# Attention and residual kernel on one core: how the inverse softmax sums reach the layout of the values product

## The chip, the cores and the metric

The kernel runs on one core of one Trainium2 chip. The metric is the device time of one execution in microseconds (us); lower is better. The engines are named as in the profile: PE (TensorE, with PEld for its weight loads), DVE (VectorE), ACT (ScalarE), POOL (GpSimd) and SP (SyncE, which issues the DMAs).

## The reference

The input x has 4 batches of 1024 rows of 1024. Rows are normalised (RMS), scaled and shifted from a condition, multiplied by `W_qkv`, and split into 16 heads of 64. What matters here is the attention of a head:

```python
q = _rms_norm(q, g_q)
k = _rms_norm(k, g_k)
logits = jnp.einsum('bhqd,bhkd->bhqk', q, k) * d ** (-0.5)
attn = jax.nn.softmax(logits, axis=-1)
o = jnp.einsum('bhqk,bhkd->bhqd', attn, v)
o = jnp.swapaxes(o, 1, 2).reshape(b, n, dim)
return o + o @ W_out
```

The result is added to x, a causal convolution of 4 taps over the rows follows with its own residual, and that is the output. The kernel applies the division of the softmax after the product with v: each row q of a head is multiplied by the inverse of its sum of exponentials. The change concerns only the path of these inverses.

## The kernel before, in words

After a short preparation (weights scaled and split into two fp16 halves) the work runs in U = 32 **units**, one for each batch and pair of heads, numbered u = 0 to 31. Every large product is made of three fp16 products, of high and low halves. A unit has 8 **steps** p; step p treats 128 query rows of both heads. In a step:

- PE makes the scores of the two heads (`score`, L958), 128 x 1024 each, into two halves of the PSUM tile `scores`. It waits there until ACT has read the scores of the step before (`exp_done`).
- DVE takes the row maxima (`maximum`, L1558) and from them the bias (L1561), for one head after the other.
- ACT takes the exponentials with their row sums in `total` (`exponent`, L1201), both heads, and then the high halves (`high`, L1209), both heads.
- DVE makes the low halves (`low`, L1567), both heads, and SP transposes the pair by DMA into `pT` (L762).

Two steps form a **group** g = 0 to 3 (256 rows of two heads, four columns of sums: two blocks of rows `a` times two heads `h`). When a group's probabilities are transposed, PE multiplies them with v (`attend`, L977, in two parts of 24 matmuls each). Its output is `values[:, 0:256]` in PSUM: the 64 columns of a head lie on 64 partitions, the 256 query rows along the free dimension. So the inverses, which DVE has with the query rows on partitions (`inv`, 128 x 4), have to be turned and repeated over the 64 partitions of each head. Before the change this goes as follows, for each of the 128 groups:

1. `invert` on DVE, at steps p = 2, 4 and 6 (and p = 0 of the next unit): reciprocal (L1668), scaled high half in fp16 (L1671), low half (L1673), in `inv_pair`.
2. `inverses` on PE, at the next odd step: two fp16 transposes (L992) into 4 partitions of `values`, seen as fp16.
3. `inverse_rows` on ACT, at the start of the same odd step: copy of 4 x 256 to `inv_row` (L1269). The first part of `attend` on PE waits for it (`inv_ev`).
4. The second part of `attend`, one step later, ends with one matmul more (L984): the 0/1 matrix `sel` (4 x 128) times `inv_row` adds the halves and repeats each head's row over its 64 partitions, in `values[:, 256:512]`.
5. `read_inverses` on ACT, at even steps between the exponentials and the high halves: 128 x 256 to `inv_all` (L1275).
6. `scale_values` on DVE, just before `low`: `oT = values * inv_all` (L1682). ACT and POOL split `oT` into halves (L1285, L1503), and SP stores them.

What else a unit carries is placed by the same hand-written order on each engine. PE makes the q, k and v products of unit u + 1 in pieces (`project`, L1016, four or five steps of a unit) with transposes of the halves of q and k (`stacks`, L1028), and from unit 8 on the products with `W_out` of unit u - 8 (`out_product`, L1050, with L1056 adding x) and float32 transposes of the result (`out_transposes`, L1068, four at a time). DVE normalises q and k (L1589, L1593), and from unit 8 on does the convolution (L1707, L1710, L1714). POOL does powers (L1474) and low halves (L1479, L1488, L1503). In units 1 to 7 PE has little beside the attention in steps 5 to 7; from unit 8 on it has a `W_out` product there. Each engine runs its own instructions in the written order, and waits in it hold everything behind them.

The functions that the diff touches follow.

## Time and profile before

| what | value |
|---|---|
| median of 3 runs (each: 2477.67, 2477.79, 2483.67) | 2477.79 us |
| span of the profiled execution, first to last instruction | 2476.2 us |
| PE busy | 2362.7 us (95%), 20794 matmuls |
| DVE busy | 2089.6 us (84%) |
| ACT busy | 1825.8 us (74%) |
| POOL busy | 641.1 us (26%) |
| PE on the chain that ended last | 64% |
| DVE on that chain | 20% |

The profiled execution's time as a run is not listed apart; its span is 1.5 to 1.6 us below the two runs that agree, which is what lies around the span. Busy times are sums over all stages. The page adds for each engine where in the span it is busy, the chain of work that ended last, and the groups of instructions with their mean durations. Matmuls overlap their successors, so the duration of one (0.2 to 0.4 us) is longer than the step from one to the next; the steps are read from the chain and the timeline.

### The profile page before, as it was taken

The page shows a single profiled execution, that of the slowest core. Times are in us where ns is not written, and L with a number is a line of the kernel's source. Part 1 is how long each engine was busy: PE and PEld are TensorE (multiplying, and loading weights), DVE is VectorE, ACT ScalarE, POOL GpSimd, SP SyncE. Part 2 cuts the span into 40 slices and gives each one's busy share as a digit, 9 for nine tenths or more (in the row PEclk, how much of TensorE's full clock was granted, in tenths as well). Part 3 has the DMA queues.
Part 4 walks back from the last instruction along what each step waited for, and adds up shares of the span by engine and source line. Part 5 has one row for each costly group of instructions (what it writes and reads, how often), then busy time and mean ns, then how long its engine had stood idle before and what let it go on. Part 6 is the DMA issues. An engine that isn't in the chain of part 4 may idle for free.

```text
span 2476.2 us, 54245 instructions
## 1 busy us (share of the span) xinstructions
PE 2362.7 (95%) x20794; PEld 1524.8 (62%) x20794; DVE 2089.6 (84%) x3368; ACT 1825.8 (74%) x2834; POOL 641.1 (26%) x451
## 2 busy tenths in 40 slices
PE   4799998999899999999999999999999999999899
PEld 0455555555466666666666666666666666666688
DVE  7769888888778888888888888888888888888876
ACT  5477778888777777877777787777777777777732
POOL 1132232332233222333332223233212222221100
PEclk9899999999999999999999999999999999999999
DMA  9999999999998989999999999999988888889971
GB/s 360 311 217 223 192 183 194 180 193 224 201 196 181 197 182 213 181 199 223 201 213 182 210 186 196 184 191 228 202 174 170 180 172 163 171 166 173 182 188 52
DMA packets 1234737, 484.99 MB, mean 196 GB/s; under 512 B 1139632, under 2 KB 1197872, under 8 KB 1232048
## 3 DMA queue, kind: packets, MB, share of 16 engines
q1 hardware_dynamic: 1234480, 481.53, 92.4%
q8 instruction: 166, 2.72, 0.5%
q14 instruction: 91, 0.75, 0.1%
HBM read 137.20 MB, written 56.66 MB: 78 GB/s over the span
## 4 chain that ended last, share of the span: by engine, by line
PE 64%; DVE 20%; issue 5%; ACT 4%; SPq 2%; DMA 1%; POOL 0%; ACTq 0%; POOLq 0%
PE proj L1016 33%; PE scores L958 10%; DVE neg L1558 9%; PE values L977 9%; PE proj L1050 8%; DVE p_pair L1567 7%; ACT p_pair L1209 3%; DVE bias L1561 2%; PE proj L1056 1%; PE misc L1068 1%; SPq L762 1%; ACT late L1201 1%; DMA w_sb<-w_dram 1%; PE values L992 1%; PE values L984 1%
## 5 line engine op out<-in xcount | busy, mean ns | idle before, releaser
L1016 PE MATMUL proj<-w_sb,xn_sb 128*128 128x384 f16 x6144 | 1035.2, 327 | 20.8 <-DMA w_sb<-w_dram 13.2
L1201 ACT ACTIVATE late<-scores,bias,l_scale 128x1024 f32<-128x1024 f32 x512 | 615.6, 1203 | 344.9 <-DVE bias L1561 325.8
L1016 PEld LDWEIGHTS proj<-w_sb,xn_sb 128*128 128x128 f16 x6144 | 587.2, 98 | 425.4 <-issue 25.9
L1567 DVE TENSOR_TENSOR p_pair<-late,p_pair 128x1024 f16<-128x1024 f32 x512 | 616.2, 1245 | 124.9 <-ACT p_pair L1209 124.8
L1558 DVE TENSOR_REDUCE neg<-scores 128x1 f32<-128x1024 f32 x512 | 623.0, 1217 | 107.0 <-PE scores L958 103.6
L1209 ACT ACTIVATE p_pair<-late 128x1024 f16<-128x1024 f32 x512 | 510.9, 1050 | 0.0
L977 PE MATMUL values<-pT,v_pair 128*64 128x256 f16 x6144 | 389.7, 277 | 14.6 <-ACT inv_row L1269 14.6
L958 PE MATMUL scores<-late 64*128 64x512 f16 x3072 | 376.1, 378 | 15.0 <-ACT late L1201 12.9
L977 PEld LDWEIGHTS values<-pT,v_pair 128*64 128x64 f16 x6144 | 319.0, 111 | 94.1 <-issue 70.3
L1474 POOL TENSOR_TENSOR rs<-ms,power 128x16 f32<-128x16 f32 x63 | 183.1, 2906 | 404.1 <-DVE ms L1581 403.7
L1050 PE MATMUL proj<-late,wo 128*128 128x256 f16 x2304 | 267.7, 273 | 1.3 <-issue 1.3
L1503 POOL TENSOR_TENSOR oT_pair<-oT,oT_pair 128x256 f16<-128x256 f32 x124 | 144.4, 1164 | 461.0 <-ACT oT_pair L1285 461.0
L958 PEld LDWEIGHTS scores<-late 64*128 64x128 f16 x3072 | 128.9, 94 | 195.7 <-issue 45.6
L1050 PEld LDWEIGHTS proj<-late,wo 128*128 128x128 f16 x2304 | 220.5, 98 | 31.5 <-issue 1.6
L1479 POOL TENSOR_TENSOR qk_pair<-stage,qk_pair 128x512 f16<-128x512 f32 x126 | 145.4, 1174 | 330.4 <-ACT qk_pair L1232 330.4
L1714 DVE SCALAR_TENSOR_TENSOR late<-late,taps 128x256 f32<-128x256 f32 x324 | 157.1, 485 | 11.6
L1217 ACT ACTIVATE stage<-proj 128x384 f32<-128x384 f32 x256 | 122.2, 477 | 29.8 <-PE proj L1016 29.8
L1269 ACT ACTIVATE inv_row<-values 4x256 f16<-4x256 f16 x128 | 46.9, 366 | 119.2 <-PE values L992 119.2
L1561 DVE TENSOR_SCALAR bias<-neg,l_scale 128x1 f32<-128x1 f32 x512 | 109.7, 214 | 18.1
L1499 POOL TENSOR_TENSOR pair<-x_in,pair 128x1024 f16<-128x1024 f32 x24 | 66.2, 2757 | 206.5 <-ACT pair L1263 199.5
L1201 ACT ACTIVATION_READ_ACCUMULATOR late<-scores,bias,l_scale 128x1 f32 x512 | 98.5, 192 | 0.0
L1050 PE MATMUL proj<-xn_sb,wo 128*128 128x256 f16 x744 | 86.5, 273 | 1.2 <-ACT late L1307 1.2
(183 smaller groups left out, 2023.6 us busy)
## 6 DMA issues: line engine op xcount, KB each, us to landing
w_sb<-w_dram SPq DMA_DIRECT2D x121, 384.0 KB, 4.1
o_dram<-oT_pair SPq DMA_DIRECT2D x124, 128.0 KB, 2.4
out<-late SPq DMA_DIRECT2D x54, 256.0 KB, 2.9
x_in<-in_x SPq DMA_DIRECT2D x25, 512.0 KB, 4.6
late<-in_x SPq DMA_DIRECT2D x25, 512.0 KB, 4.1
wq_raw<-in_L_cond_W_qkv SPq DMA_DIRECT2D x8, 1536.0 KB, 11.2
late<-o_dram SPq DMA_DIRECT2D x12, 1024.0 KB, 6.1
xn_dram<-late SPq DMA_DIRECT2D x21, 512.0 KB, 3.6
```

Of the source, the lines that this page charges most:

```text
L958: last = nc.tensor.matmul(scores[:, h, n * HN:(n + 1) * HN], stack[rows_, par, i, p * P:(p + 1) * P], stack[rows_, par, j, n * HN:(n + 1) ...
L977: last = nc.tensor.matmul(values[DH * h:DH * h + DH, 0:QG].rearrange("p (a n) -> p a n", a=2), v_pair[:, par, 2 * c + h, DH * i:DH * i + D ...
L1016: last = nc.tensor.matmul(proj[:, t % 2, 0:6 * DH], xn_sb[:, t, i * K + c, :], w_sb[:, c, j, :], start=(c == 0 and i == j == 0), stop=(c = ...
L1050: last = nc.tensor.matmul(dst, const["wo"][:, c, b, m * P:(m + 1) * P], oT_[:, c, a, :], start=(c == 0 and a == b == 0 and c1 == K), stop= ...
L1201: nc.scalar.activation(prob[:, h, :], scores[:, h, :], ACT.Exp, bias=bias[:, s:s + 1], scale=const["l_scale"][:, 0:1], accum_out=total[:, ...
L1209: nc.scalar.activation(p_pair[:, s % 4, 0, :], prob[:, h, :], ACT.Copy).then_inc(hi_done, 1)
L1474: nc.gpsimd.tensor_tensor(rs[:], ms[:], const["power"][:, 0:4 * KH], ALU.pow).then_inc(h_pw, 1)
L1479: last = nc.gpsimd.tensor_tensor(qk_pair[:, j, 1].rearrange("p t (h d) -> p (t h) d", d=DH), stage[:, hf, :, j * DH:(j + 1) * DH], qk_pair ...
L1558: nc.vector.tensor_reduce(neg[:, s:s + 1], scores[:, h, :], axis=AX.X, op=ALU.max, negate=True).then_inc(max_done, 1)
L1561: nc.vector.tensor_scalar(bias[:, s:s + 1], neg[:, s:s + 1], const["l_scale"][:, 0:1], P_SHIFT, ALU.mult, ALU.add).then_inc(bias_done, 1)
L1567: nc.vector.tensor_tensor(p_pair[:, s % 4, 1, :], prob[:, h, :], p_pair[:, s % 4, 0, :], ALU.subtract).then_inc(lo_done, 1)
L1714: nc.vector.scalar_tensor_tensor(out=acc_[:, m, :], in0=y_[:, m, k:k + QG], scalar=const["taps"][:, k, c:c + 1], in1=acc_[:, m, :], op0=AL ...
```

## The change

DVE copies the four float32 inverses of a group into `inv_wide`, each repeated over 64 columns (128 x 256, one instruction with a broadcast source). PE turns this with two float32 transposes of 128 x 128 straight into `values[:, 256:512]`, where each head's 64 partitions now hold its row. ACT reads that to `inv_all` where it read the 4 x 256 before, and `attend` waits for this read. The halves (L1671, L1673), the copy of the rows (L1269) and the product with `sel` (L984), and the `sel` matrix itself, are gone, and `inv_all` no longer has a read of its own between exponentials and high halves.

```diff
--- before.py
+++ after.py
@@ -72,7 +72,6 @@
             wo=sb("wo", [P, K, 2, D], F16),
             eps_u=sb("eps_u", [P, U], F32),
             back=sb("back", [P, U], F32),
-            sel=sb("sel", [4, 2 * DH], F16),
             y_scale=sb("y_scale", [P, U], F32),
             carry=sb("carry", [P, U], F32),
             g_qk=sb("g_qk", [P, DH], F32),
@@ -399,10 +398,6 @@
             nc.vector.tensor_copy(smallT[:], ps_mod[:, 0:rows]).then_inc(small_c, 1)
             v.wait_ge(small_c, 1)
             v.wait_ge(eyed, 1)
-            step(nc.vector.tensor_tensor(
-                const["sel"][:].rearrange("p (h d) -> p h d", d=DH),
-                const["eye32"][0:4, 0:2].rearrange("p (h a) -> p h a", a=1).to_broadcast([4, 2, DH]),
-                const["eye32"][0:4, 2:4].rearrange("p (h a) -> p h a", a=1).to_broadcast([4, 2, DH]), ALU.add))
             step(nc.vector.tensor_copy(const["taps"][:], smallT[:, 0:B * K].rearrange("p (b c) -> p b c", c=K)))
             step(nc.vector.tensor_scalar(const["taps"][:, B - 1, :], const["taps"][:, B - 1, :], 1.0, None, ALU.add))
             step(nc.vector.tensor_copy(const["conv_b"][:], smallT[:, row_cb:rows]))
@@ -474,7 +469,6 @@
     QG = 2 * P
     TAPS = B
     H = TAPS - 1
-    INV_UP = 2.0 ** 22
     x_t = x.rearrange("b n d -> (b n) d")
     out_t = out.rearrange("b n d -> (b n) d")
     wo_v = W_out.rearrange("(c p) n -> c p n", p=P)
@@ -497,8 +491,7 @@
         v_pair = sb("v_pair", [P, 2, 2 * K, 2 * DH], F16)
         p_pair = sb("p_pair", [P, 4, 2, N], F16)
         inv = sb("inv", [P, 2, 4], F32)
-        inv_pair = sb("inv_pair", [P, 2, 2, 4], F16)
-        inv_row = sb("inv_row", [4, QG], F16)
+        inv_wide = sb("inv_wide", [P, 2, 2, P], F32)
         inv_all = sb("inv_all", [P, QG], F32)
         oT = sb("oT", [P, QG], F32)
         oT_pair = sb("oT_pair", [P, 2, QG], F16)
@@ -586,11 +579,8 @@
         pT_in = [sem(f"pT_in{i}") for i in range(8)]
         pv_done = sem("pv_done")
         inv_rc = sem("inv_rc")
-        inv_hi = sem("inv_hi")
         inv_done = sem("inv_done")
         inv_tr = sem("inv_tr")
-        inv_ev = sem("inv_ev")
-        all_mm = sem("all_mm")
         all_ev = sem("all_ev")
         o_done = sem("o_done")
         o_hi = sem("o_hi")
@@ -662,8 +652,6 @@
         first_pair = [p_pair[:, i] for i in range(4)]
         square = x_in
         last_y = scores[:, 0, 0:QG]
-
-        inv_bank = values[0:4, QG:QG + P].bitcast(F16)
 
         def odd_tail(T):
             return static(T) and T >= U - K - 1 and T % 2 == 1
@@ -965,7 +953,7 @@
             def attend(u, g, par, part):
                 n = NG * u + g
                 if part == 0:
-                    pe.wait_ge(inv_ev, n + 1)
+                    pe.wait_ge(all_ev, n + 1)
                     if g == 0:
                         pe.wait_ge(v_lo, 2 * u + 2)
                     for i in range(4):
@@ -981,16 +969,14 @@
                                 start=(c == 0 and i == j == 0), stop=(c == K - 1 and j == 1))
                 if part == 1:
                     last.then_inc(pv_done, 1)
-                    nc.tensor.matmul(values[:, QG:2 * QG], const["sel"][:], inv_row[:],
-                                     start=True, stop=True).then_inc(all_mm, 1)
 
             def inverses(u, g):
                 n = NG * u + g
                 pe.wait_ge(inv_done, n + 1)
                 need(pe, o_done, n)
                 for a in range(2):
-                    last = nc.tensor.transpose(inv_bank[:, a * P:(a + 1) * P], inv_pair[:, g % 2, a, :],
-                                               const["eye16"][:])
+                    last = nc.tensor.transpose(values[:, QG + a * P:QG + (a + 1) * P], inv_wide[:, g % 2, a, :],
+                                               const["eye32"][:])
                 last.then_inc(inv_tr, 1)
 
             def project(w, t, q0, q1, fins=None):
@@ -1262,18 +1248,11 @@
                 else:
                     nc.scalar.activation(pair_[:, 0], buffer, ACT.Copy).then_inc(x_hi, 1)
 
-            def inverse_rows(u, g):
+            def read_inverses(u, g):
                 n = NG * u + g
                 act.wait_ge(inv_tr, n + 1)
-                need(act, all_mm, n)
-                nc.scalar.activation(inv_row[:], inv_bank, ACT.Copy).then_inc(inv_ev, 1)
-
-            def read_inverses(u, g):
-                n = NG * u + g
-                act.wait_ge(all_mm, n + 1)
                 need(act, o_done, n)
-                nc.scalar.activation(inv_all[:], values[:, QG:2 * QG], ACT.Copy,
-                                     scale=1.0 / INV_UP).then_inc(all_ev, 1)
+                nc.scalar.activation(inv_all[:], values[:, QG:2 * QG], ACT.Copy).then_inc(all_ev, 1)
 
             def o_high(u, g):
                 n = NG * u + g
@@ -1329,9 +1308,9 @@
                     if last and p == 4:
                         read_y(T, T - par + 2, 1)
                     if p % 2 == 1 and p >= 3:
-                        inverse_rows(u, (p - 3) // 2)
+                        read_inverses(u, (p - 3) // 2)
                     elif p == 1 and begun:
-                        inverse_rows(u - 1, 3)
+                        read_inverses(u - 1, 3)
                     if p == 0:
                         if has_early(u):
                             read_projection(w, 1)
@@ -1361,10 +1340,6 @@
                         read_projection(w + 1, 0)
                     exponent(u, p, 0, par)
                     exponent(u, p, 1, par)
-                    if p % 2 == 0 and p >= 4:
-                        read_inverses(u, (p - 4) // 2)
-                    elif p % 2 == 0 and begun:
-                        read_inverses(u - 1, 2 + p // 2)
                     high(u, p, 0)
                     high(u, p, 1)
                     if 4 <= u < K and p in (1, 3):
@@ -1441,17 +1416,15 @@
             high_values(0, 0, 1)
             in_units(unit, act)
             scales = U - K + 2
-            read_inverses(U - 1, 2)
             read_y(U - K, scales, 0)
             read_y(U - K, scales, 1)
             o_high(U - 1, 2)
             read_y(U - K + 1, scales, 0)
-            inverse_rows(U - 1, 3)
+            read_inverses(U - 1, 3)
             read_out(U - K - 1, 0)
             read_y(U - K + 1, scales, 1)
             read_out(U - K - 1, 1)
             read_out(U - K, 0)
-            read_inverses(U - 1, 3)
             o_high(U - 1, 3)
             for T in range(U - K + 2, U):
                 read_y(T, scales, 0)
@@ -1667,12 +1640,9 @@
                 col = par * NS + 4 * g
                 nc.vector.reciprocal(inv[:, g % 2, :], total[:, col:col + 4]).then_inc(inv_rc, 1)
                 dve.wait_ge(inv_rc, n + 1)
-                one_ = inv[:, g % 2, :].rearrange("p (a h) -> p a h", a=2)
-                nc.vector.tensor_scalar(inv_pair[:, g % 2, :, 0:2], one_, INV_UP, None, ALU.mult).then_inc(inv_hi, 1)
-                dve.wait_ge(inv_hi, n + 1)
-                nc.vector.scalar_tensor_tensor(out=inv_pair[:, g % 2, :, 2:4], in0=one_, scalar=INV_UP,
-                                               in1=inv_pair[:, g % 2, :, 0:2], op0=ALU.mult,
-                                               op1=ALU.subtract).then_inc(inv_done, 1)
+                by_row = inv[:, g % 2, :].rearrange("p (a b) -> p a b", b=1).to_broadcast([P, 4, DH])
+                nc.vector.tensor_copy(inv_wide[:, g % 2].rearrange("p a (h d) -> p (a h) d", d=DH),
+                                      by_row).then_inc(inv_done, 1)
 
             def scale_values(u, g):
                 n = NG * u + g
```

In the order of PE's instructions, in a unit of the second half of the program: L977 and L965 are the values product of before and now, L958 and L946 the scores, L1016 and L1002 the q, k, v product, L1068 and L1054 the float32 transposes of the result, L992 and L978 the transposes of the inverses. Before:

```order
L958 MATMUL scores<-late 128x512 x12
L977 MATMUL values<-pT,v_pair 64x256 x24
L984 MATMUL values<-inv_row,sel 128x256
L1016 MATMUL proj<-w_sb,xn_sb 128x384 x36
L1068 MATMUL misc<-eye,late 128x128 x4
L958 MATMUL scores<-late 128x512 x12
L992 MATMUL values<-eye,inv_pair 4x128 x2
L1050 MATMUL proj<-late,wo 128x256 x24
```

Now:

```order
L946 MATMUL scores<-late 128x512 x12
L965 MATMUL values<-pT,v_pair 64x256 x24
L1002 MATMUL proj<-w_sb,xn_sb 128x384 x36
L1054 MATMUL misc<-eye,late 128x128 x4
L946 MATMUL scores<-late 128x512 x12
L978 MATMUL values<-eye,inv_wide 128x128 x2
L1036 MATMUL proj<-late,wo 128x256 x24
```

The `sel` product between the values product and the projection is gone, and the two transposes of the inverses give 128 partitions in place of 4; nothing else moved.

In the order of ACT's instructions, steps 0 and 1 of a unit (L1201 and L1187 are the exponentials, L1209 and L1195 the high halves, L1285 and L1264 the high half of `oT`). Before:

```order
L1201 ACTIVATE late,total<-scores,bias,l_scale 128x1024 x2
L1275 ACTIVATE inv_all<-values 128x256
L1209 ACTIVATE p_pair<-late 128x1024 x2
L1285 ACTIVATE oT_pair<-oT 128x256
L1217 ACTIVATE stage<-proj 128x384
L1269 ACTIVATE inv_row<-values 4x256
L1217 ACTIVATE stage<-proj 128x384
L1201 ACTIVATE late,total<-scores,bias,l_scale 128x1024 x2
L1209 ACTIVATE p_pair<-late 128x1024 x2
L1263 ACTIVATE pair<-x_in 128x1024
```

Now:

```order
L1187 ACTIVATE late,total<-scores,bias,l_scale 128x1024 x2
L1195 ACTIVATE p_pair<-late 128x1024 x2
L1264 ACTIVATE oT_pair<-oT 128x256
L1203 ACTIVATE stage<-proj 128x384
L1255 ACTIVATE inv_all<-values 128x256
L1203 ACTIVATE stage<-proj 128x384
L1187 ACTIVATE late,total<-scores,bias,l_scale 128x1024 x2
L1195 ACTIVATE p_pair<-late 128x1024 x2
L1249 ACTIVATE pair<-x_in 128x1024
```

The read of `inv_all` stands where the copy to `inv_row` stood, and nothing stands between the exponentials and the high halves.

## Rows read from the trace of the kernel before

**Rows 1.** Busy us in units 9 to 30 by engine (PE, PEld, DVE, ACT, POOL), clock, DMA.
```profile
738.30:2311.40 1573.10, 1571.68 (x14168) 1031.12 (x14166) 1360.55 (x2180) 1214.01 (x1905) 433.96 (x294) 1.00 0.94 189
```

**Rows 2.** The chain, units 15 and 16: start us, length us, what.
```profile
1205.86 0.21 PE values L984
...
1212.02 0.44 PE misc L1068 x4
...
1213.86 0.20 PE values L992 x2
...
1217.24 2.62 PE proj L1050 x24
...
1220.31 0.45 PE misc L1028 x8
...
1236.01 1.47 PE scores L958 x12
...
1307.55 1.47 PE scores L958 x12
```

**Rows 3.** Timeline, TensorE near the end: start us, us, instruction, idle before.
```profile
2387.38 0.66 PE L1068 MATMUL misc<-eye,late 128*128 128x128 f32 x4
2387.97 1.50 PE L977 MATMUL values<-pT,v_pair 128*64 128x256 f16 x24
```

**Rows 4.** Groups by line: shapes, count, busy us, mean ns, idle before and releaser.
```profile
L1275 ACT ACTIVATE inv_all<-values 128x256 f32<-128x256 f32 x128 | 47.6, 372 | 1.0 <-PE values L984 1.0
L1269 ACT ACTIVATE inv_row<-values 4x256 f16<-4x256 f16 x128 | 46.9, 366 | 119.2 <-PE values L992 119.2
...
L1707 DVE TENSOR_SCALAR late<-late,taps,conv_b 128x256 f32<-128x256 f32 x108 | 43.9, 407 | 0.0
```

**Rows 5.** The tile inv_pair: durations in ns, least, median, most.
```profile
L1671 DVE TENSOR_SCALAR inv_pair<-inv x128: 169/169/1143, 156.6 to 2372.9; 128x4 f16<-128x4 f32 x128
L1673 DVE SCALAR_TENSOR_TENSOR inv_pair<-inv,inv_pair x128: 161/163/1076, 156.8 to 2373.1; 128x4 f16<-128x4 f32 x128
```

**Rows 6.** Timeline of unit 15 from step 6 on, to the first scores of the next.
```profile
1222.56 0.98 PEld L958 LDWEIGHTS scores<-late 64*128 64x128 f16 x12 [0.20 <-issue]
...
1225.25 2.27 POOL L1479 TENSOR_TENSOR qk_pair<-stage,qk_pair 128x512 f16<-128x512 f32 x2 [4.12 <-ACT qk_pair L1232]
...
1227.04 0.51 DVE L1671 TENSOR_SCALAR inv_pair<-inv 128x4 f16<-128x4 f32 x1
...
1227.48 1.15 POOL L1488 TENSOR_TENSOR v_pair<-stage,v_pair 128x512 f16<-128x512 f32 x1
1227.58 1.07 DVE L1673 SCALAR_TENSOR_TENSOR inv_pair<-inv,inv_pair 128x4 f16<-128x4 f32 x1
...
1228.58 0.41 DVE L1682 TENSOR_TENSOR oT<-values,inv_all 128x256 f32<-128x256 f32 x1
...
1229.50 2.36 DVE L1567 TENSOR_TENSOR p_pair<-late,p_pair 128x1024 f16<-128x1024 f32 x2 [0.51 <-ACT p_pair L1209]
...
1236.00 0.98 PEld L958 LDWEIGHTS scores<-late 64*128 64x128 f16 x12 [0.33 <-ACT late L1201]
```

**Rows 7.** The chain in unit 4: with the read of inv_all, without it, with invert.
```profile
404.31 0.06 ACT inv_all L1275
...
404.48 1.06 ACT p_pair L1209
...
413.63 0.95 ACT p_pair L1209
...
436.17 0.18 DVE inv L1668
...
436.37 0.18 DVE inv_pair L1671
...
436.58 0.16 DVE inv_pair L1673
```

**Rows 8.** A stretch of unit 5, columns as in Rows 1.
```profile
507.20:510.40 3.20, 3.20 (x31) 2.47 (x30) 3.13 (x5) 2.98 (x5) 3.20 (x4) 0.50 1.06 198
```

## The prediction

> **What bounds the kernel now.** I read the page first, then the chain that ended last, cut by stages, then the timeline of single steps, and the groups by line for durations. The chain over the whole span lies mostly on PE and a fifth on DVE, but that mixes two regimes.
>
> From unit 9 to unit 30, 1573.1 us for 22 units, PE is busy for 1571.7 us at a granted clock of 1.00, while DVE has 1360.6 and ACT 1214.0 [rows 1]. The unit's period is the distance between two first scores, 1307.55 - 1236.01 = 71.54 us [rows 2]. PE waits once in it for another engine: the first scores of a unit wait for the last exponentials on ACT, and PEld sits idle for 0.33 us there; before scores that wait for nobody it sits 0.20 us [rows 6], so the wait proper is 0.13 us. The reader is to see that PE is the bound, and that a second path, over DVE and ACT, is only 0.13 us longer than PE's own at one place. Unit 8 is much the same without the wait.
>
> In units 1 to 6 the chain runs almost wholly over DVE and ACT: maxima, bias, exponentials, high halves, low halves. PE's work counts little there. Units 0 and 7, and unit 31 with the tail, are mixed.
>
> **The change on PE.** Gone: one `sel` product a group. On the chain it takes 0.21 us, of which a product with as many columns takes 0.11 elsewhere (24 `W_out` products of 256 columns in 2.62 us) [rows 2]; the rest is paid when PE goes from one shape of the array to another. Leaving the values product costs its own step either way, so I count all of the 0.21.
>
> Changed: two fp16 transposes, 0.20 us on the chain [rows 2], become two float32 ones of 128 x 128. The nearest rows are the float32 transposes of the result. Four of them take 0.44 us on the chain where the fourth is followed by scores (whose step in is counted elsewhere) [rows 2]: 0.11 each. Four between two values products take 2387.97 - 2387.38 = 0.59 us [rows 3], which is 0.15 more: part for the first, whose weights PE has not loaded ahead, and 0.09 for going back to the values' shape. The inverses come behind scores, so they pay the first part; a projection or `W_out` product follows, of the same shape, so they don't pay the second. Two take 0.59 - 2 x 0.11 - 0.09 = 0.28 us (the 0.09 is what the change of shape adds to the fp16 pair: 0.20 less two bare steps of 0.056, from eight such transposes in 0.45 us [rows 2]). Bounds: 0.22 (nothing for the first) and 0.37 (both). I take 0.28.
>
> Sum for PE in one unit: 4 x (-0.21 + 0.28 - 0.20) = -0.52 us; with the bounds -0.76 and -0.16.
>
> **The change on ACT.** The copy to `inv_row` (0.366 us, 128 times) becomes the read to `inv_all`, which cost 0.372 in its old place [rows 4]: nothing. PE's values product then waits for a read as long as before. In the steady units the `W_out` product or projection lies between transposes and values product, so this stays covered; without that cover it would cost the 0.006 of the difference. The read between exponentials and high halves goes. On the chain the high half ends at 404.48 + 1.06 = 405.54 with the read in between, 1.23 us after the 404.31 at which the exponentials were through; without it, it takes 0.95 [rows 7]. So the path over ACT gets 0.28 us shorter in each even step. What is late next is DVE: in step 6 it has been idle for 0.51 us before the low half [rows 6], so the 0.28 arrives in full.
>
> At the one place where PE waits, the path over DVE and ACT gets 0.28 shorter, and PE's own path between the same two ends 0.13 (one `sel` product less, one pair of transposes 0.08 longer). The wait is then 0.13 - 0.28 + 0.13, about nothing: the 0.13 goes too.
>
> **The change on DVE.** Two small instructions, 0.17 and 0.16 us when nothing is in the way [rows 5] and 0.20 and 0.18 with the gap behind each, go; one copy of 256 float32 columns comes. No such copy is in the trace. Below it lie the small instructions themselves at 0.16 us, above it a one-input operation over 256 float32 columns at 0.41 [rows 4]. A copy needs no scalars, which makes it shorter than the 0.41, but 256 columns need time: I take 0.32, nearest to the upper row. Against the 0.38 that goes this is nothing, in the bounds -0.2 to +0.05 us a group. In steady units DVE has slack; where it has none it counts twice a unit at most (8 times in units 1 to 6 the halves are on the chain, one of them in [rows 7]).
>
> The trace shows what can stretch it. In step 6 of unit 15 the high half took 0.51 us and the low half 1.07, both ending with a POOL operation that ran beside them: L1479, from 1225.25 for 2.27 us, and L1488, from 1227.48 for 1.15 [rows 6]. Units 9 to 30 all do this in group 2. The copy starts at the same 1227.04, so it waits for the first, to 1227.52, and is over by about 1227.9; DVE would be free 0.7 us earlier than now. The page "SBUF — State Buffer" of the Trainium skill (section "SBUF: two separate sides") has a rule that speaks against the copy: a two-port DVE operation and GpSimd lock each other out for a whole instruction, whichever starts first. The trace agrees: 0.51 and 1.07 us against 0.17 and 0.16. By that rule the copy could also lose to the second POOL operation; that is rival B.
>
> **Sum.** Units 9 to 30: 22 x (0.52 + 0.13) = 14.3 us. Unit 8: 0.5. Units 1 to 6: the read of `inv_all` is on the chain 14 times (one of them in [rows 7]), 14 x 0.28 = 3.9, the copy nothing. Units 0 and 7: half of PE's sum each, 0.5 together. Unit 31: the read is on the chain three times, 0.8; tail: one `sel` product, 0.2. Together 20.2 us, from a span of 2476.2: 2456.0. The two runs that agree lie 1.6 above the span; the forecast is 2457.6 us against the median of 2477.8.
>
> **Rivals.**
>
> B. *The copy is held behind POOL.* In step 6 it waits to 1228.63, where L1488 ends, ends at about 1228.95, and the scaling of the values (0.41, at 1228.58 now) at 1229.36. Now the low half starts at 1229.50 [rows 6]; instead of 0.28 the path gains 0.14. The wait of 0.13 stays: 22 x 0.13 = 2.9 us less gain, 2460.5. With 0.41 for the copy it is 22 x 0.09 more: 2462.5. For it: POOL starts L1488 within 0.1 us of the end of L1479. Against it: now, too, the first of DVE's two got in between them.
>
> C. *The saved product is paid elsewhere.* If the 0.21 is a price of changing the array's shape that the next projection must pay anyway, only 0.11 a group goes, and with 0.37 for the transposes the sum is 4 x (0.17 - 0.11) = +0.24 a unit against the 0.13 of the wait: 22 x 0.11 = +2.4 us, less 5 elsewhere: 2475, no change. Against it: the values product before `sel` pays its own change already.
>
> D. *Slower: PE's clock falls.* In unit 5, after a pause of PE, 3.2 us ran at a granted clock of 0.50 [rows 8], that is 1.2 in place of 2.4 GHz; in the steady units it is 1.00 [rows 1]. A stretch like this costs 1.6 us of PE's work; one in each of 23 units costs 37 us, and the time would be 2494. It decides from some 17 such stretches in all, (20.2 + 7.4) / 1.6. For it, the page "TensorE: Matmul & The Clock Gate" (Part 4, PE-mode transpose) of the Trainium skill says that transposes don't count as PE's being busy as matmuls do, and the new ones last longer. Against it: eight float32 transposes and 32 fp16 ones already stand in each steady unit, and the clock there is 1.00; the change adds no pause.
>
> E. *DMA or another queue takes the gain.* SP's order is untouched, and PE has no wait for `pT` in the steady units; the DMA share there is 0.94 [rows 1], the one thing for it. It would leave half the gain: 2468.
>
> **How the numbers follow.** Forecast 0.74, B 0.11, C 0.06, D 0.03, E 0.06. The bounds of the transposes alone move the steady sum: with 0.22 each pair PE gives 0.24 a unit more, but only where the path over DVE lets it, some 0.18: -4 us; with 0.37 it is 0.36 less: +8 us. The copy's bounds add 1 or 2. The range goes from 2451 to 2467, which takes in B and leaves out C, D and half of E. A measurement of this kernel tells 0.3%, 7.4 us, from no change; the limit is 2470.4. Faster: the forecast, B and E, 0.91; same: C, 0.06; slower: D, 0.03.
>
> **What would show it.** The period of a steady unit at 70.9 us; PEld's idle before a unit's first scores back at 0.20; the transposes of the inverses at 0.27 to 0.28 us on the chain, and the projection straight behind the values product; one DVE copy of about 0.32 us, with one stretched to 0.8 in group 2; 47 us less busy on ACT. A period of 71.5 with a new wait on PE, or a clock under 1.00 after unit 8, would make it wrong.

## The result, and the profile after

| | before | after |
|---|---|---|
| median (lowest to highest) | 2479.74 us (2477.67 to 2483.67), 4 runs | 2457.59 us (2456.85 to 2462.56), 4 runs |
| span of the profiled execution | 2476.2 us | 2454.9 us |
| ratio after / before | | 0.9916, 95% interval 0.9904 to 0.9928 |

The changed kernel is faster by 0.8%, 22 us in the medians and 21.3 us in the spans. The page after:

```profile
span 2454.9 us, 53605 instructions
PE 2337.2 (95%) x20666; PEld 1529.3 (62%) x20666; DVE 2061.2 (84%) x3239; ACT 1797.1 (73%) x2706; POOL 648.6 (26%) x451
...
PE 72%; DVE 11%; SPq 4%; issue 3%; ACT 2%; DMA 2%; POOL 1%; ACTq 0%; POOLq 0%
```

PE's share of the chain that ended last rose from 64% to 72% and DVE's fell from 20% to 11%. The small waits at which the chain used to leave PE are gone, so it stays on PE. PE is 25.5 us less busy.

The same stretch as in [rows 1], units 9 to 30, in the table of busy times (PE, PEld, DVE, ACT and POOL with their instruction counts, then granted clock, DMA share and GB/s):

```profile
734.80:2291.00 1556.20, 1555.44 (x14080) 1037.49 (x14077) 1336.56 (x2092) 1194.29 (x1817) 439.08 (x294) 1.00 0.95 191
```

The 22 units take 1556.2 us where they took 1573.1: 16.9 of the 21.3 us are here. The granted clock is still 1.00. The period by two first scores of units 15 and 16 in the timeline:

```profile
1297.39 1.47 PE L946 MATMUL scores<-late 64*128 64x512 f16 x12
...
1368.12 1.47 PE L946 MATMUL scores<-late 64*128 64x512 f16 x12
```

That is 70.73 us against 71.54; the median of units 9 to 22 is 70.70 against 71.54. The chain of the kernel before shows one pair of the old transposes and the projection behind it:

```profile
1246.05 1.40 PE scores L958 x12
1247.45 0.20 PE values L992 x2
1247.65 5.96 PE proj L1016 x36
```

and the chain after shows two odd steps and the end of a values product in the even step between them (`values` L978 are the new transposes, L965 is the values product):

```profile
1165.82 1.40 PE scores L946 x12
1167.22 0.37 PE values L978 x2
1167.59 5.85 PE proj L1002 x36
1173.44 0.44 PE misc L1054 x4
...
1195.53 1.43 PE values L965 x24
1196.96 5.96 PE proj L1002 x36
1202.91 0.44 PE misc L1054 x4
```

No matmul stands between the values product and the projection any more (L984 in [rows 2]). The new pair takes 0.37, but the projection behind it 5.85 where 5.96 stood behind the old pair.

The tile `inv_wide` (count, then shortest, median and longest in ns), and DVE and POOL in step 6 of a steady unit, where [rows 6] had the two halves at 0.51 and 1.07:

```profile
L1644 DVE COPY inv_wide<-inv x128: 293/294/776, 158.9 to 2351.7; 128x256 f32<-128x256 f32 x128
```

```profile
1216.33 2.27 POOL L1452 TENSOR_TENSOR qk_pair<-stage,qk_pair 128x512 f16<-128x512 f32 x2 [4.32 <-ACT qk_pair L1218]
1217.99 0.77 DVE L1644 COPY inv_wide<-inv 128x256 f32<-128x256 f32 x1
1218.56 1.21 POOL L1461 TENSOR_TENSOR v_pair<-stage,v_pair 128x512 f16<-128x512 f32 x1
1218.68 0.41 DVE L1652 TENSOR_TENSOR oT<-values,inv_all 128x256 f32<-128x256 f32 x1
1220.18 2.36 DVE L1540 TENSOR_TENSOR p_pair<-late,p_pair 128x1024 f16<-128x1024 f32 x2 [1.09 <-ACT p_pair L1195]
...
1226.69 0.98 PEld L946 LDWEIGHTS scores<-late 64*128 64x128 f16 x12 [0.21 <-ACT late L1187]
```

The copy is stretched to 0.77 by the first POOL pair, which ends at 1218.60, and is over at 1218.76; L1461, which starts at 1218.56 beside its end, takes 1.21 where L1488 took 1.15. DVE then idles 1.09 us before the low half (0.51 before), and PEld's idle before the next unit's scores is 0.21, down from 0.33.

Where the 21.3 us of the span came from, with a unit counted from its first scores: 16.9 in units 9 to 30; 0.7 in unit 8 (70.5 to 69.8); 2.4 in units 0 to 7 (528.6 to 526.2); 1.0 in unit 31 and the tail; 0.3 ahead of unit 0. Counted from DVE's first row maximum instead, where the window of [rows 1] begins, units 0 to 7 go from 528.6 to 527.4 and unit 8 from 72.2 to 70.3: in unit 8 of the changed kernel DVE is still at a low half when the scores are ready and takes up the maximum 1.2 us later, so 1.2 us change sides. What a unit takes of PE's time is read from the scores.

The period is not the same in all 22 units. In the kernel before it is 71.54 up to unit 23 and 71.42 from unit 24 on, here units 26 and 27:

```profile
1951.14 1.47 PE L958 MATMUL scores<-late 64*128 64x512 f16 x12
2022.56 1.47 PE L958 MATMUL scores<-late 64*128 64x512 f16 x12
```

In the changed kernel it is 70.70 before and behind unit 23. So the change gives 0.84 us in each of units 9 to 22 and 0.72 in each of units 24 to 30; the section on the prediction says why.

### The profile page after: what moved, and what is told of

It reads as the page before. It is cut to its first block, busy times and chain, and to the rows that moved or that the text cites. A ratio compares the mean times of both kernels' runs of the same rounds, so it can differ in the third digit from the quotient of the medians.

```text
span 2454.9 us, 53605 instructions
## 1 busy us (share of the span) xinstructions
PE 2337.2 (95%) x20666; PEld 1529.3 (62%) x20666; DVE 2061.2 (84%) x3239; ACT 1797.1 (73%) x2706; POOL 648.6 (26%) x451
## 4 chain that ended last, share of the span: by engine, by line
PE 72%; DVE 11%; SPq 4%; issue 3%; ACT 2%; DMA 2%; POOL 1%; ACTq 0%; POOLq 0%
PE proj L1002 32%; PE proj L1036 12%; PE scores L946 11%; PE values L965 11%; DVE p_pair L1540 4%; DVE neg L1531 4%; SPq L750 3%; PE proj L1042 2%; PE values L978 1%; ACT p_pair L1195 1%; DMA w_sb<-w_dram 1%; PE misc L1054 1%; PE misc L1014 1%; PE proj L1014 1%; SPq L706 1%
## 5 line engine op out<-in xcount | busy, mean ns | idle before, releaser
L1002 PE MATMUL proj<-w_sb,xn_sb 128*128 128x384 f16 x6144 | 1034.1, 327 | 26.4 <-DMA w_sb<-w_dram 18.2
L1002 PEld LDWEIGHTS proj<-w_sb,xn_sb 128*128 128x128 f16 x6144 | 592.8, 98 | 431.3 <-issue 50.4
L1187 ACT ACTIVATE late<-scores,bias,l_scale 128x1024 f32<-128x1024 f32 x512 | 615.9, 1204 | 332.6 <-DVE bias L1534 313.7
L1195 ACT ACTIVATE p_pair<-late 128x1024 f16<-128x1024 f32 x512 | 510.0, 1046 | 0.0
L965 PE MATMUL values<-pT,v_pair 128*64 128x256 f16 x6144 | 385.3, 275 | 13.2 <-ACT inv_all L1255 13.2
L946 PE MATMUL scores<-late 64*128 64x512 f16 x3072 | 376.1, 378 | 18.1 <-ACT late L1187 17.6
L965 PEld LDWEIGHTS values<-pT,v_pair 128*64 128x64 f16 x6144 | 316.4, 110 | 91.8 <-issue 70.1
L946 PEld LDWEIGHTS scores<-late 64*128 64x128 f16 x3072 | 128.9, 94 | 197.8 <-issue 45.0
L1452 POOL TENSOR_TENSOR qk_pair<-stage,qk_pair 128x512 f16<-128x512 f32 x126 | 147.1, 1189 | 327.2 <-ACT qk_pair L1218 327.2
L1255 ACT ACTIVATE inv_all<-values 128x256 f32<-128x256 f32 x128 | 48.9, 382 | 139.0 <-PE values L978 138.9
L1187 ACT ACTIVATION_READ_ACCUMULATOR late<-scores,bias,l_scale 128x1 f32 x512 | 98.6, 193 | 0.0
```

The lines of the kernel that those rows point to most:

```text
L946: last = nc.tensor.matmul(scores[:, h, n * HN:(n + 1) * HN], stack[rows_, par, i, p * P:(p + 1) * P], stack[rows_, par, j, n * HN:(n + 1) ...
L965: last = nc.tensor.matmul(values[DH * h:DH * h + DH, 0:QG].rearrange("p (a n) -> p a n", a=2), v_pair[:, par, 2 * c + h, DH * i:DH * i + D ...
L1002: last = nc.tensor.matmul(proj[:, t % 2, 0:6 * DH], xn_sb[:, t, i * K + c, :], w_sb[:, c, j, :], start=(c == 0 and i == j == 0), stop=(c = ...
L1187: nc.scalar.activation(prob[:, h, :], scores[:, h, :], ACT.Exp, bias=bias[:, s:s + 1], scale=const["l_scale"][:, 0:1], accum_out=total[:, ...
L1195: nc.scalar.activation(p_pair[:, s % 4, 0, :], prob[:, h, :], ACT.Copy).then_inc(hi_done, 1)
L1452: last = nc.gpsimd.tensor_tensor(qk_pair[:, j, 1].rearrange("p t (h d) -> p (t h) d", d=DH), stage[:, hf, :, j * DH:(j + 1) * DH], qk_pair ...
```

## The experiments

All but the control, `after_again`, are edits of the changed kernel; line numbers of one kernel can differ by a few from the next. "Period" is the median of units 9 to 22, from first scores to first scores. Each ratio is taken to runs of the kernel before beside that kernel (medians 2478.99 to 2479.97).

| run | median us (runs) | ratio to before (95%) | period us |
|---|---|---|---|
| before | 2479.74 (4) | | 71.54 |
| after | 2457.59 (4) | 0.9916 (0.9904 to 0.9928) | 70.70 |
| after_again | 2455.93 (4) | 0.9903 (0.9888 to 0.9918) | 70.70 |
| e1_sel_shape_back | 2477.17 (11) | 0.9985 (0.9973 to 0.9997) | 71.52 |
| e2_full_shape_product | 2466.01 (5) | 0.9948 (0.9935 to 0.9961) | 71.12 |
| e3_read_between | 2471.68 (5) | 0.9968 (0.9956 to 0.9980) | 71.30 |
| e4_copy_twice | 2456.30 (6) | 0.9901 (0.9886 to 0.9917) | 70.70 |
| e5_both_parts_together | 2448.97 (4) | 0.9877 (0.9863 to 0.9892) | 70.46 |
| e6_turn_behind_piece | 2453.93 (4) | 0.9896 (0.9882 to 0.9911) | 70.65 |
| e7_both | 2449.57 (4) | 0.9874 (0.9857 to 0.9890) | 70.42 |
| e8_pool_behind_copy | 2484.40 (10) | 1.0018 (1.0007 to 1.0028) | 71.98 |

**The price of the product with `sel`.** It is put back as a product of the same shape that leads to nothing: 4 x 128 weights, 256 columns, at the end of the second part of `attend`.

```diff
                 if part == 1:
-                    last.then_inc(pv_done, 1)
+                    nc.tensor.matmul(values[:, QG:2 * QG], const["eye16"][0:4, 0:P],
+                                     const["eye16"][0:4, 8:9].to_broadcast([4, QG]),
+                                     start=True, stop=True).then_inc(pv_done, 1)
```

> The changed kernel with one more fp16 product behind each group's values product, of the same size as the one that was removed (4 rows x 128 columns of weights, 256 columns), into the part of the PSUM tile that has already been read. Its result is not used. My theory (the steady units 9 to 30 are bound by PE, and the removed product cost 0.21 us a group, half of it for changing the array's shape): the period goes from 70.70 back to about 71.5 us, the time to about 2477 us. Rival, only its 256 columns cost: 0.11 a group, 2467 us. Rival, the gain came from ACT's read and PE's product was beside the path: 2458 to 2460 us.

The second kernel has the same product with weights of 128 x 128, `const["eye16"][:]`.

> The same, but the extra product has 128 rows x 128 columns of weights, the shape of the projection behind it. My theory: no shape is changed on its account, so it costs 0.107 us a group, 0.43 a steady unit: period 71.1 us, time 2467 us. If a product costs 0.21 there whatever its shape: 71.5 and 2477 us. If PE is not the bound: 2458 us.

Periods 71.52 and 71.12: the small shape costs 0.82 us a unit, 0.21 a group, and the full shape 0.42, 0.11 a group. The chain of the first, then of the second:

```profile
1204.09 0.21 PE values L971
1204.30 5.96 PE proj L1004 x36
```

```profile
1198.58 0.22 PE values L971
1198.80 5.85 PE proj L1004 x36
```

The 0.21 or 0.22 of the product itself is the same in both rows. The reader is to see the projection behind it: 5.96 behind a 4-row product, and behind the values product in the changed kernel, but 5.85 behind a full-shape one. So the 4-row product paid one change of shape of its own, and left the next one for the projection; the full-shape product paid the change that the projection would have paid. Rival C said that only 0.11 of the 0.21 would go because the projection pays the change anyway; the first run shows all of the 0.21 gone. It shows one thing more: with the product kept, the change would have been worth nothing in units 9 to 22 (71.52 against 71.54), and would have cost 0.10 in units 24 to 30 (71.52 against 71.42).

**The read between exponentials and high halves.** An ACT copy of the same size, from SBUF where the read was from PSUM, whose result nothing reads, goes back to the old place in the even steps; it took 0.403 us.

```diff
                     exponent(u, p, 0, par)
                     exponent(u, p, 1, par)
+                    if p % 2 == 0 and (p >= 4 or begun):
+                        nc.scalar.activation(spare_all[:]...,
+                                             const["eye32"][:]....to_broadcast([P, 2, P]), ACT.Copy)
                     high(u, p, 0)
                     high(u, p, 1)
```

> The changed kernel with an unused ACT copy of 128 x 256 float32 between the exponentials and the high halves of each even step, where the read of the inverses stood before. My theory: it lengthens the path over DVE and ACT by 0.28 to 0.3 us an even step; in a steady unit this counts once, where the first scores wait for the last exponentials, since that path and PE's own are within 0.05 us of each other now: period +0.25 us, 5 to 6 us in 22 units, and 3 to 4 more in units 1 to 6, so 2466 to 2468 us. Rival, the read was what the change was worth: 2476 us. Rival, ACT has slack everywhere: 2458 us.

The median is 2471.68, some 4 us above what was expected; the period went up by 0.60. The waits of units 9 to 30 (total us, times, longest), before, after and in this run:

```profile
PEld scores L958 <- ACT late L1201: 7.2, 22, 0.3
PEld misc L1068 <- DVE late L1714: 4.0, 14, 0.3
```

```profile
PEld scores L946 <- ACT late L1187: 4.6, 22, 0.2
PEld misc L1054 <- DVE late L1684: 2.2, 13, 0.2
PE proj L1002 <- DMA w_sb<-w_dram: 0.6, 1, 0.6
```

```profile
PEld scores L947 <- ACT late L1188: 11.3, 22, 0.5
PEld misc L1055 <- DVE late L1689: 7.1, 15, 0.5
PE scores L947 <- ACT late L1188: 5.4, 22, 0.2
```

Two waits answer to the read, not one: by the steps of the timeline the first scores come 0.30 later than after the change, and the transposes of the result in step 1 0.30. The second is for DVE's convolution, which stands behind the low halves, which stand behind ACT's high halves. Before the change it was there already, with PEld idle 4.0 / 14 = 0.29 us; after it is 2.2 / 13 = 0.17. The prediction knew only of the first. In this run both are longer than before the change: the spare copy takes 0.403 us where the read took 0.372, PE's own work is shorter, and so both paths over ACT stick out more. In units 24 to 30, where no transpose of the result waits for DVE in any of the three profiles, the same read costs once: the period is 71.00 there, 0.30 over 70.70. Units 0 to 7 took 531.5 us, 5.3 more than in the profile after, 6 to 7 more than in most of the others (see below): in this one profile the read does cost there.

**The copy on DVE.** It is issued twice, the first time into a spare tile.

```diff
+                nc.vector.tensor_copy(spare_wide[:].rearrange("p a (h d) -> p (a h) d", d=DH), by_row)
                 nc.vector.tensor_copy(inv_wide[:, g % 2].rearrange("p a (h d) -> p (a h) d", d=DH),
                                       by_row).then_inc(inv_done, 1)
```

> The changed kernel with the wide DVE copy issued twice (the first time into a tile that nobody reads). My theory: DVE has slack in the steady units, also in group 2, where the copy stands behind POOL: period 70.7 us unchanged, or up to 0.2 more if the second copy is caught by the second POOL operation; in units 1 to 6 some 8 copies of 0.3 us on the chain: 2460 us, at most 2464. Rival, DVE is the bound: 128 x 0.3 = 38 us more, 2495 us.

> The changed kernel once more, beside the next three on one chip: 2457 to 2458 us, period of the steady units 70.70 us. Units 0 to 7 took 527.4 us in its first profile and 528.6 in the kernel before, where I had expected 4.4 us less. If that was scatter between executions of the first units, this one shows 524 to 525; if the gain isn't there, 527 again.

The period is 70.70 in all three, and the medians of 2456.30, 2455.93 and 2457.59 lie as close as runs of one kernel do. A second copy of 0.29 us a group costs nothing that can be measured. In group 2 it was even caught by the second POOL operation, which is what rival B said of the one copy:

```profile
1219.29 0.77 DVE L1645 COPY spare_wide<-inv 128x256 f32<-128x256 f32 x1
1219.87 1.20 POOL L1462 TENSOR_TENSOR v_pair<-stage,v_pair 128x512 f16<-128x512 f32 x1
1219.98 1.25 DVE L1646 COPY inv_wide<-inv 128x256 f32<-128x256 f32 x1
```

The two copies use up DVE's idle time before the low half, 1.09 us in the changed kernel, and the low half still starts 3.85 us behind the first POOL operation, as it does there. So what rival B feared costs nothing here, and not the 0.13 us a unit that it was priced at.

**Fewer changes of shape.** If a change of the array's shape costs 0.1 us, then a place with one change fewer should pay. In units 8 to 31 the second part of `attend` of two of the four groups moves from behind the next step's scores to directly behind the first part: the order values, scores, values, projection becomes values, scores, projection.

```diff
-                    if p % 2 == 0 and p >= 4:
+                    if p % 2 == 0 and p >= 4 and not (outs and p == 4):
                         attend(u, (p - 4) // 2, par, 1)
-                    elif p % 2 == 0 and begun:
+                    elif p % 2 == 0 and begun and p < 4 and not (outs and p == 2):
                         attend(u - 1, 2 + p // 2, 1 - par, 1)
...
                     if p % 2 == 1 and p >= 3:
                         attend(u, (p - 3) // 2, par, 0)
+                        if outs and p == 3:
+                            attend(u, 0, par, 1)
                     elif p == 1 and begun:
                         attend(u - 1, 3, 1 - par, 0)
+                        if outs:
+                            attend(u - 1, 3, 1 - par, 1)
```

> The changed kernel with, in units 8 to 31, the second part of the values product of two of the four groups directly behind the first part, ahead of the next step's scores and not behind them. It saves one change of the array's shape, 0.09 us, twice a unit. My theory (PE's steps add up to the period, and the changes of shape are part of them): period 70.70 - 0.19 = 70.51 us, time 2453 us. Rival: the scores of steps 2 and 4 now come 1.4 us later, which DVE has to wait for, and the path over DVE and ACT takes the gain back: 70.7 or more, 2458 to 2465 us.

The period is 70.46, the median 2448.97. In the chain the 48 products stand in one piece:

```profile
1170.61 2.74 PE values L965 x48
1173.35 1.40 PE scores L946 x12
1174.75 6.93 PE proj L1002 x42
```

2.74 us against 2 x 1.43 = 2.86. That is 0.12 a place, two places a unit, 0.24: 70.70 - 70.46. It is the price of one change of shape, which the prediction read from [rows 3] as 0.09.

**The first transpose behind a piece of the projection.** At steps 1 and 3 of units 8 to 30 six projection products go ahead of the transposes, so that their weights can be loaded ahead.

```diff
+                    behind = outs and qkv and p in (1, 3)
...                  (inverses not ahead of the projection where behind)
-                        for t, q0, q1 in (...)[p]:
+                        for i, (t, q0, q1) in enumerate((...)[p]):
+                            if behind and i == 0:
+                                project(w, t, q0, q0 + 1, T - 1 if fins else None)
+                                inverses(*((u - 1, 3) if p == 1 else (u, 0)))
+                                q0 += 1
...
```

> The changed kernel with the two float32 transposes of a group behind the first six matmuls of the projection in steps 1 and 3 of units 8 to 30, and not right behind the scores. My theory: the first transposes took 0.165 us and the second 0.109 because the first's weights can't be loaded while the array has the scores' shape; behind a projection both take 0.109. Period 70.70 - 0.11 = 70.59 us, time 2455 us. Rival: ACT, which waits for the transposes at the head of its step, gets them 1 us later and so does the rest of the step: no gain, or 1 to 2 us more a unit where DVE has no slack, up to 2480 us.

```profile
1179.65 1.08 PE proj L1002 x6
1180.73 0.22 PE values L978 x2
1180.95 4.88 PE proj L1002 x30
```

The pair takes 0.22 there, two bare steps of 0.11, the lower bound of the prediction. But the saving is 0.37 + 5.85 - (1.08 + 0.22 + 4.88) = 0.04 us a place: the change of shape is now paid by the projection, and only the longer first step of the transposes, 0.165 instead of 0.109, was saved. The period is 70.65, where I had expected 70.59. In units 24 to 30 it is 70.61, the whole of two places; in units 9 to 22 the transposes of the result in step 1, which wait for DVE there, take back 0.04. Both edits together:

> Both of these edits together. If PE's steps add: period 70.70 - 0.30 = 70.40 us, time 2450 to 2451 us. If the path over DVE and ACT is then longer than PE's, the period stays where the better of the two alone is.

Period 70.42, median 2449.57, the fastest by the period and equal to e5 by the median. In its profile units 15 and 23, in which PE waits for weights from DRAM, took 71.5 us, 1.1 more than the others. It beats the kernel before by 1.3% (1.1 to 1.4) and the changed kernel by 6 us (against the control's 2455.93) to 8 us.

**POOL behind the copy.** POOL's low half of q and k at step 6 waits until the copy of group 2 is done, so that the copy can't be stretched.

```diff
                     if p == 6 and qkv:
+                        if outs:
+                            pool.wait_ge(inv_done, NG * u + 3)
                         half_low(w, 1)
```

> The changed kernel with one more wait on POOL: in step 6 of units 8 to 31 its low halves of q and k start only when the wide copy of group 2 is done. Theory on the port: the copy of group 2 takes 0.77 us in 21 or 22 units, and 0.29 in nearly all other groups, only because it starts while a POOL operation runs, and ends 0.29 us behind that one's end; now all of group 2 take 0.29. POOL's two operations start some 2 us later, at about the time at which they end now, and PE's transposes need them 2.5 us after that: the period stays at 70.70 us, the time at 2456 to 2458 us. Rival: the copy is long in group 2 for another cause (0.77 stays). Rival: the low halves come too late for PE's transposes in step 7: period up to 1 us more, 2478 us.

The copy now takes 0.29 in group 2 as elsewhere, and the kernel is slower than the one before: 2484.40, ratio 1.0018 (1.0007 to 1.0028), period 71.98, 1.28 more than after. Its timeline at the same place:

```profile
1227.30 0.29 DVE L1646 COPY inv_wide<-inv 128x256 f32<-128x256 f32 x1
1227.67 2.28 POOL L1452 TENSOR_TENSOR qk_pair<-stage,qk_pair 128x512 f16<-128x512 f32 x2 [6.34 <-DVE inv_wide L1646]
1229.49 3.64 DVE L1542 TENSOR_TENSOR p_pair<-late,p_pair 128x1024 f16<-128x1024 f32 x2 [1.57 <-ACT p_pair L1195]
1229.91 2.14 POOL L1461 TENSOR_TENSOR v_pair<-stage,v_pair 128x512 f16<-128x512 f32 x1
1237.28 1.47 PE L946 MATMUL scores<-late 64*128 64x512 f16 x12 [1.22 <-ACT late L1187]
```

POOL's work now falls on DVE's low halves. The pair of them takes 3.64 us instead of 2.36, and POOL's L1461 2.14 instead of 1.21. The low halves are on the path to the next unit's first scores, for which PE now waits 1.22 us; the copy never was. In the changed kernel the stretched copy stands in idle time and takes the meeting with POOL that would otherwise hit the low halves. No value expected ahead of the run had this cost: that the copy would be short was right, what the delayed POOL work does to the low halves was not priced.

## Why the prediction was right

The forecast was 2457.6 and the median is 2457.59, but that is closer than its terms were, and so luck: the steady units gave 2.6 us more than forecast, the first units 2.0 less in the profile after, and the forecast gain of 20.2 was taken off a median before of 2477.8, which is 2479.74 with the fourth run. The gain in the medians is 22.2, in the spans 21.3.

| term | predicted | measured |
|---|---|---|
| `sel` product, a group | -0.21 | -0.21 (e1: 0.82 / 4) |
| transposes, a group | +0.08 | +0.07 |
| wait before the first scores, a unit | -0.13 | -0.12 (PEld idle 0.33 to 0.21) |
| second wait, step 1 of a unit | not seen | -0.11 in units 9 to 22, nothing in units 24 to 30 |
| units 9 to 30 | -14.3 | -16.9 |
| unit 8 | -0.5 | -0.7 |
| units 0 to 7 | -4.4 | -2.4 in this profile, -3 to -4 in most |
| unit 31, tail | -1.0 | -1.0 |

**Right: what bounds the kernel, and the product with `sel`.** The steady period is PE's work, and a product less on PE is a product's time less. Taking all of the 0.21 was right, and rival C wrong, by the first experiment.

**Right in size, wrong in reading: the transposes.** I said 0.28 for a pair on the chain. It shows 0.37, my upper bound. Step by step, from one start to the next in the timeline: the old pair has 0.306 from the last scores to the first transpose, 0.055 to the second and 0.151 to the projection; the new one 0.307, 0.165 and 0.109. The way in from the scores costs the same in both. The old pair, with only 4 columns, is followed by a second change of shape (0.151 where a bare step is 0.056), the new one, of the projection's own shape, is not, but its two steps are longer. The chain charges the way in to the pair and the way out to the projection: 0.20 + 5.96 for the old, 0.37 + 5.85 for the new, a difference of 0.06, or 0.07 by the steps (0.581 against 0.512). I took the saved 0.09 of the way out off the pair, 0.59 - 0.22 - 0.09, where it does not stand; it came off the projection. The sum was nearly right (+0.08), the sign to look for in the profile (0.27 to 0.28 on the chain) was wrong. What to compare is the sum over the pair and the piece behind it.

**Missed: the second wait.** The step "PE waits once in it for another engine" was wrong. The transposes of the result in step 1 waited too, for DVE's convolution; the trace names this wait in 14 of 22 units, and the prediction took up the largest wait only. Step by step in unit 12, these transposes and the way into them take 0.11 less after the change. The kernel before shows the same by itself: from unit 24 on the trace names no such wait, those steps are 0.12 shorter than in unit 12, every other kind of step of PE is the same, and the period is 71.42 and not 71.54. After the change the steps are as short in both stretches. So units 24 to 30 gain 0.72 and units 9 to 22 gain 0.84. In unit 12 the four groups give -0.83 + 0.28 = -0.55 us, the first wait -0.12, the second -0.11; the 0.05 that are left of 0.83 lie in steps between products that the change doesn't touch, a few ns on some, and why they are shorter stays open.

**Half right: units 1 to 6.** I gave them 14 x 0.28 = 3.9 us for the read on the chain. With the 0.5 for units 0 and 7 that makes 4.4; the profile after shows 2.4 for units 0 to 7. In the first units PE's wait for weights grew between the two profiles (total, times, longest, from 130 to 670 us, before and after):

```profile
PE proj L1016 <- DMA w_sb<-w_dram: 13.2, 11, 2.2
```

```profile
PE proj L1002 <- DMA w_sb<-w_dram: 17.6, 11, 3.9
```

Units 0 to 7, from first scores to first scores, took 524.4, 525.1, 524.8, 525.7, 525.6 and 525.4 in six further profiles (the control, e1, e2, e5, e7, e8), 526.9 in e4 and 520.0 in e6. Against 528.6, of which there is one profile, that is a gain of 3 to 4 with a scatter as large. With the extra read of e3 they took 531.5, 6 to 7 more than in those six. The 3.9 is thus neither confirmed nor refuted; that DMA takes a part of it, as rival E had it, fits the row above, but no run shows it: the control has as long a wait (17.4) and took 1.8 us less than the profile after.

**Right: the copy and the read.** 0.294 against my 0.32 in the open, 0.77 against 0.8 in group 2, not held by L1461: rival B did not come true, and in e4, where the second copy was held, it cost nothing. One side of the POOL rule that I weighed is seen in e8: the low halves, with two inputs from SBUF, are stretched as well, from 2.36 to 3.64, by L1452 and L1461, the counterparts of the two POOL lines of [rows 6]. The Trainium skill ("SBUF — State Buffer", section "SBUF: two separate sides") states that a DVE operation with two inputs from SBUF and a GpSimd operation that reads SBUF hold a shared port for the whole instruction, and that the later one waits. The trace agrees: the first low half is over at 1231.03, L1461 1.02 behind it at 1232.05, and the second low half 1.08 behind that, at 1233.13. The sign of 47 us less busy on ACT was read against the wrong number: the page's busy time fell by 28.7, since it counts instructions that overlap once (added up one by one, ACT's instructions are 48.0 us less). In the groups by line (count, total busy, mean ns) it is there:

```profile
L1255 ACT ACTIVATE inv_all<-values 128x256 f32<-128x256 f32 x128 | 48.9, 382 | 139.0 <-PE values L978 138.9
```

48.9 us stand where 46.9 + 47.6 stood before, 45.6 less.

**Right: no slower rival.** The granted clock is 1.00 in units 9 to 30, with eight float32 transposes more in each unit: rival D did not come. Rival E came in one unit, the 23rd, by 0.7 us in the profile after (see the last section).

The errors in the span: 2.6 us too little in the steady units, 0.2 in unit 8 and 0.3 ahead of unit 0, against 2.0 too much in the first units. With the first units as predicted the span would have been 2.0 us less.

## What to carry to other kernels

Where PE bounds a stage, count the changes of the array's shape, not only the products: here a small product between two shapes cost 0.21 us where a full-shape one cost 0.11, and putting two values products side by side gave another 7 to 9 us. Read a short piece of the chain together with the piece behind it. And before a stretched instruction is freed, ask what stands in its place: the copy that met POOL cost nothing, while the low halves that met it after the edit cost 1.28 us a unit.

## What the hardware showed that was not expected

- Two values products of 24 with scores between them cost 0.12 us more than the same 48 in one piece (2 x 1.43 - 2.74), one change of shape.
- Two DVE operations with both inputs in SBUF (L1542 of e8) took 3.64 us beside POOL instead of 2.36, and POOL's L1461 2.14 instead of 1.21: they hold each other up in both directions, by turns.
- In one place after the change, unit 23, the last before the next batch, PE waited for weights from DRAM for 0.6 us; in the control run of the same kernel the same wait was 2.3. The kernel before shows none there. Unit 23 took 71.42 and 74.89 us in these two profiles, where the units around it took 70.70, and 75.15 in e6. It goes with the speed of PE: in the four profiles with a period of 71.30 or more (before, e1, e3, e8) unit 23 is no longer than the units around it, in the seven with 71.12 or less it is longer by 0.5 to 4.5 us. What a faster PE reaches next is the weights, here in the control:

```profile
PE proj L1002 <- DMA w_sb<-w_dram: 2.3, 1, 2.3
```
